# A non-local attention block: order of work in the first step of each image

## Chip, cores and metric

One core of a Trainium2 chip. The metric is the device time of one execution in microseconds (us), the median of several runs. The core has five engines that run their own instruction queues and meet at semaphores: TensorE (PE; its weight loads, PEld, are listed apart), VectorE (DVE), ScalarE (ACT), GpSimd (POOL) and SyncE (SP), which here only issues DMAs.

## The reference

Eight images `x` of 128 channels and 32 x 32 pixels, so N = 1024 tokens. Three 1x1 convolutions to 64 channels, attention without a scale over the tokens of one image, a 1x1 convolution back to 128 channels, batch normalisation with fixed statistics, and a residual:

```python
g     = (einsum('bchw,oc->bhwo', x, w_g) + b_g).reshape(B, N, Ci)
theta = (einsum('bchw,oc->bhwo', x, w_theta) + b_theta).reshape(B, N, Ci)
phi   = (einsum('bchw,oc->bohw', x, w_phi) + b_phi[:, None, None]).reshape(B, Ci, N)
att   = softmax(einsum('bnc,bcm->bnm', theta, phi), axis=-1)
y     = einsum('bnm,bmc->bnc', att, g).reshape(B, H, W, Ci)
out   = einsum('bhwc,oc->bohw', y, w_out) + b_out[:, None, None]
inv   = bn_gamma / sqrt(bn_var + 1e-5)
return x + out * inv[:, None, None] + (bn_beta - bn_mean * inv)[:, None, None]
```

## The kernel before

**Tiles.** The attention is worked in 64 tiles of 128 query rows, 8 per image (`MT = 8`); a half is four tiles (512 columns, one PSUM bank). A tile's row of 1024 scores is held in one of two double banks `ps_scores`. Per tile: `scores` (L727) makes it with four matmuls from parts of theta and phi that are stored as high and low (`theta_hl`, `phi_hh`, `phi_ll`); VectorE takes the negated row maximum (`row_maximum`, L591, and for three tiles of eight a small addition, L596); ScalarE takes the exponential with that bias and sums the row (L544, `probs`, a ring of four). Then the tile has to be transposed and split in a high and a low fp16 part, `pt_hi` and `pt_lo`. Tiles at places 1, 5 and 7 of an image are split by GpSimd (L422, L426) and transposed by DMA (`turn_hi`, `turn_lo`, L302 and L311). The other five are transposed by TensorE with the identity into two banks `ps_flip` (L792, eight transposes), and read from there by ScalarE, which writes the high part in two instructions (L532), and by VectorE, which writes the low part in two (L692: scaled source minus high part).

**Per half.** `sum_high` (L739, eight matmuls) and `sum_low` (L746, eight) accumulate attention times g in `ps_y`. VectorE scales the sum to `y_norm` (`scale_y`, L608), TensorE multiplies it by the output weights (`convolve`, L753, into `ps_misc`), VectorE adds the residual (`add_residual`, L601), and SP stores.

**Per image, for the next image.** theta and phi are projected in two halves into the same bank `ps_misc` (L826, three matmuls each, at j = 0 and 1). ScalarE takes each out to `qk` (L518, at j = 1 and 2, semaphore `proj_out`); the second projection waits for the first evacuation. GpSimd splits `qk` (L402, L407) and SP restacks the parts with six DMAs (L292). g is projected at j = 4 (L711); its largest value is spread over the partitions by a transpose (L733, at j = 7) and read by VectorE at j = 0 (L585), and small operations make scales of it (L664 to L670). At j = 0 VectorE also inverts the row sums of a half (L635) and scales two of them (L639).

**Order.** Every compute engine has a function `step(it, k)`, called for k = 0, 1, ... up to the last tile and a few steps on, with `j = k % 8`; in step k TensorE makes scores of tile k + 1 and transposes tile k - 2, ScalarE takes the exponential of tile k and the high parts of tile k - 2, and VectorE the maximum of tile k + 1 and the low parts of tile k - 2. The queues are in order, and the order inside a step is the order in which `step` lists the work. Steps 8 to 55 are a loop of three turns of 16 steps, which so begin at images 1, 3 and 5. GpSimd has its own function of the same kind. SP issues by a list written out per image (`image`).

**In the first step of an image (j = 0)**, tile k is tile 0 of the new image and tile k - 2 is tile 6 of the one before. ScalarE: high parts of tile 6 once TensorE has transposed it, then the exponential of tile 0. VectorE: the peak, the sums, the scales, the low parts of tile 6, the maximum of tile 1. TensorE: transposes of tile 6, scores of tile 1, first projection. At j = 1: scores of tile 2 (they wait for exponential 0, as the two are in the same banks: `wait(pe, probs_ready, t - 1)`), second projection, `sum_low` of the last image's first half. At j = 2: transposes of tile 0 (they wait for the low parts of tile 6: `wait(pe, pt_lo_ready, 2 * f + c - 1)`), scores of tile 3, `convolve`.

Of the kernel before, what the change touches and what calls it, by code (L numbers as in the profile page):

```python
# [23 lines left out]
def build_nonlocal_attention(nc, x, w_tp_t, w_g_t, w_out_t, channel_vectors, out):  # L24
# [9 lines left out]
    ALU = mybir.AluOpType  # L34
    ACT = mybir.ActivationFunctionType
# [5 lines left out]
    P = 128  # L41
    BANK = 512
    EPS = 1e-5
    PROB_SCALE = 2.0 ** 15
# [27 lines left out]
    with ExitStack() as ctx:  # L72
# [152 lines left out]
        def by_dma(it, k):  # L225
            return k % MT in BY_DMA and not in_last_half(tile_at(it, k))
# [257 lines left out]
        @block.scalar  # L484
        def _(act):
            def evacuate_g(b, source, target):
                wait(act, g_split, b - 1)
                nc.scalar.activation(target, source, ACT.Copy).then_inc(g_out, 1)

            def scale_y(h, r, source, cols):  # L490
                act.wait_ge(y_ready, h + 1)
                nc.scalar.activation(y_norm[:, cols], source, ACT.Copy,
                                     scale=y_unit[:, r:r + 1]).then_inc(y_scaled, 1)

            act.dma_start(w_tp[:, :], w_tp_t).then_inc(w_tp_in, 16)
# [12 lines left out]
            act.wait_ge(g_ready, 1)  # L508
            evacuate_g(0, ps_flip[0][:, :], g_raw[0][:, :, :].rearrange("p t c -> p (t c)"))

            def step(it, k):
                image, j = image_at(it, k), k % MT

                if j in (1, 2) and exists(image + 1, B):
                    c = j - 1
                    act.wait_ge(proj_ready, 2 * image + c + 1)
                    wait(act, lo_ready, 2 * image)
                    nc.scalar.activation(qk[:, c * BANK:(c + 1) * BANK], ps_misc[:, :], ACT.Identity,  # L518
                                         bias=BIAS_TP).then_inc(proj_out, 1)

                if j == 5 and exists(image + 1, B):
                    act.wait_ge(g_ready, image + 2)
                    evacuate_g(image + 1, ps_misc[:, :], g_raw[(k // MT + 1) % 2][:, :, :].rearrange("p t c -> p (t c)"))

                t = tile_at(it, k - 2)
                if exists(t, TILES) and not by_dma(it, k - 2):
                    slot, ring = (k - 2) % HALF_TILES, (k - 2) // HALF_TILES % 2
                    if slot == 0:
                        wait(act, y_ready, half_at(it, k - 2) - 1)
                    for c in range(2):  # L530
                        act.wait_ge(flipped, 2 * flip_at(it, k - 2) + c + 1)
                        nc.scalar.activation(  # L532
                            pt_hi[ring][:, c * HALF_TILES:(c + 1) * HALF_TILES, slot * P:(slot + 1) * P],
                            ps_flip[c][:, :].rearrange("p (a n) -> p a n", n=P),
                            ACT.Copy, scale=PROB_SCALE).then_inc(pt_hi_ready, 1)

                t = tile_at(it, k)
                if exists(t, TILES):
                    act.wait_ge(max_ready, t + 1)
                    if by_dma(it, k - PROB_RING):  # L540
                        wait(act, p_lo_ready, move_at(it, k - PROB_RING) + 1)
                    else:
                        wait(act, flipped, 2 * flip_at(it, k - PROB_RING) + 2)
                    nc.scalar.activation(probs[k % PROB_RING][:, :], ps_scores[k % 2][:, :], ACT.Exp,  # L544
                                         bias=neg_max[:, k % STEPS:k % STEPS + 1],
                                         accum_out=row_sum[:, k % STEPS:k % STEPS + 1]).then_inc(probs_ready, 1)

            run_steps(act, step)
            act.wait_ge(conv_ready, HALVES - 1)
            scale_y(HALVES - 1, 1, ps_y[:, LAST_PIECES[0]], LAST_PIECES[0])  # L550
            scale_y(HALVES, 1, ps_scores[0][:, 0:P], LAST_PIECES[1])

        @block.vector
        def _(dve):
# [49 lines left out]
            def scale_y(h, half, r, image, spread):  # L604
# [13 lines left out]
            nc.vector.scalar_tensor_tensor(out=SHIFT, in0=BIAS_SUM, scalar=INV, in1=BETA_SHIFT,  # L618
                                           op0=ALU.mult, op1=ALU.add).then_inc(shift_ready, 1)

            def step(it, k):
                image, j = image_at(it, k), k % MT

# [58 lines left out]
                                                   scalar=g_factor[:, 0:1], in1=g_parts[0][:, :, 0:CI],  # L682
                                                   op0=ALU.mult, op1=ALU.subtract).then_inc(g_split, 1)

                t = tile_at(it, k - 2)
                if exists(t, TILES) and not by_dma(it, k - 2):
                    slot, ring = (k - 2) % HALF_TILES, (k - 2) // HALF_TILES % 2
                    for c in range(2):
                        where = (slice(None), slice(c * HALF_TILES, (c + 1) * HALF_TILES),
                                 slice(slot * P, (slot + 1) * P))  # L690
                        dve.wait_ge(pt_hi_ready, 2 * flip_at(it, k - 2) + c + 1)
                        nc.vector.scalar_tensor_tensor(  # L692
                            out=pt_lo[ring][where], in0=ps_flip[c][:, :].rearrange("p (a n) -> p a n", n=P),
                            scalar=PROB_SCALE, in1=pt_hi[ring][where],
                            op0=ALU.mult, op1=ALU.subtract).then_inc(pt_lo_ready, 1)
                t = tile_at(it, k + 1)
                if exists(t, TILES):
                    row_maximum(it, k + 1)

            run_steps(dve, step)  # L700
            dve.wait_ge(resid_ready, B)
# [5 lines left out]
        def _(pe):  # L707
# [68 lines left out]
            def step(it, k):  # L776
# [18 lines left out]
                        last.then_inc(flipped, 1)  # L795

                h, quarter = half_at(it, k - 6), (k - 6) % HALF_TILES
                if quarter == 1 and exists(h, HALVES - 2):
                    ring, r = ring_of(k - 6), (k - 6) // MT % 2
                    pe.wait_ge(pt_lo_ready, 2 * flip_at(it, k - 7 + HALF_TILES))  # L800
                    pe.wait_ge(hi_moved[ring], moved_by(it, k - 6))
                    pe.wait_ge(g_split, image_at(it, k - 6) + 1)
                    wait(pe, y_scaled, h)
                    sum_high(ring, r, ps_y, slice(0, BANK), slice(0, BANK))

                t = tile_at(it, k + 1)
                if exists(t, TILES):
                    scores(t, it, k + 1)


                image, j = image_at(it, k), k % MT
                more = exists(image + 1, B)
                if j in (0, 1) and more:
                    if j == 0:
# [24 lines left out]
                    wait(pe, result_ready, 2 * image - 1)  # L839
                    project_g(ps_misc, (k // MT + 1) % 2, range(MT)).then_inc(g_ready, 1)  # L840


                h, quarter = half_at(it, k - 6), (k - 6) % HALF_TILES
                if exists(h, HALVES - 2):
                    ring, r = ring_of(k - 6), (k - 6) // MT % 2
                    if quarter == 3:
                        pe.wait_ge(lo_moved[ring], moved_by(it, k - 6))
                        sum_low(ring, r, ps_y, slice(0, BANK), slice(0, BANK))

                if tile_is(it, k, 1):  # L850
                    spread_peak(0, 0, ps_y[:, 0:P])
# [58 lines left out]
```

## Time and profile before

| | us |
|---|---|
| median of 3 runs | 208.63 (208.4 to 208.84) |
| the profiled execution | 210.12 |
| its span | 208.2 |
| PE busy | 196.0 (94%) |
| DVE busy | 178.3 (86%) |
| ACT busy | 136.3 (65%) |
| POOL busy | 152.5 (73%) |
| DMA, mean | 169 GB/s |

The span is the part of the profiled execution from its first to its last instruction; all rows below are times within it. The granted TensorE clock is full throughout (0.997 in the mean).

How to read it: a busy share is a mean over stages, and TensorE's ends are modelled. A row of the timeline has its start, its duration (of all instructions merged in it), engine, line, operation, output and inputs, shapes, count, and in brackets the idle time of that engine ahead of it with what ended the idle time. The chain is the work that ended last, followed back from the last instruction.

### The profile page before, as it was taken

How to read it: one execution, taken by the hardware profiler on the slowest of the kernel's cores; microseconds unless marked ns; L12 is line 12 of the kernel's file. 1: busy time of each engine (PE TensorE's matmuls, PEld its weight loads, DVE VectorE, ACT ScalarE, POOL GpSimd, SP SyncE). 2: the span in 40 equal slices, each digit the busy share in tenths (PEclk: the TensorE clock that was granted, in tenths of full speed). 3: DMA queues.
4: the chain of work that ended last, by engine and by line, in shares of the span. 5: the costliest groups of instructions: out<-in, count | busy, mean ns of one | idle time of the engine just before them, and what ended most of it. 6: DMA issues, size and time to landing. Idle time of an engine off the chain costs nothing.

```text
span 208.2 us, 3966 instructions
## 1 busy us (share of the span) xinstructions
PE 196.0 (94%) x1100; PEld 133.4 (64%) x1100; DVE 178.3 (86%) x291; ACT 136.3 (65%) x245; POOL 152.5 (73%) x127
## 2 busy tenths in 40 slices
PE   7997999999999989899999999999999998999993
PEld 6575765695666746477566856677566955566542
DVE  0689899979997898988997899878998899989861
ACT  2766867867676655676577766766577666667721
POOL 2538898699779996499987999699888965864400
PEclk9999999999999999999999999999999999999998
DMA  5215978999999999899979987899988997839211
GB/s 162 85 51 161 215 149 128 250 223 179 217 113 248 210 141 200 97 279 207 223 171 261 229 196 161 189 233 211 159 191 180 219 169 159 150 55 135 70 41 63
DMA packets 59500, 35.28 MB, mean 169 GB/s; under 512 B 50400, under 2 KB 50912, under 8 KB 59488
## 3 DMA queue, kind: packets, MB, share of 16 engines
q1 hardware_dynamic: 59200, 35.01, 81.9%
q10 hardware_dynamic: 288, 0.14, 0.2%
q14 instruction: 7, 0.06, 0.2%
q8 instruction: 5, 0.08, 0.2%
HBM read 8.36 MB, written 4.23 MB: 60 GB/s over the span
## 4 chain that ended last, share of the span: by engine, by line
PE 60%; DVE 17%; issue 7%; ACT 6%; DMA 5%; SPq 1%; POOL 1%; ACTq 0%; DVEq 0%; POOLq 0%
PE ps_scores L727 18%; PE ps_y L739 11%; PE ps_flip L792 10%; DVE neg_max L591 6%; PE ps_misc L753 6%; PE ps_misc L711 5%; DVE pt_lo L692 5%; PE ps_y L746 5%; DMA pt_hi<-p_hi 4%; ACT probs L544 4%; PE ps_scores L765 2%; DMA w_tp<-w_tp_t_dram 2%; ACT pt_hi L532 2%; PE ps_misc L826 1%; DVE y_norm L608 1%
## 5 line engine op out<-in xcount | busy, mean ns | idle before, releaser
L544 ACT ACTIVATE probs<-ps_scores,neg_max 128x1024 f32<-128x1024 f32 x64 | 71.7, 1120 | 34.3 <-DVE neg_max L596 25.5
L591 DVE TENSOR_REDUCE neg_max<-ps_scores 128x1 f32<-128x1024 f32 x64 | 78.0, 1218 | 8.9 <-PE ps_scores L727 8.4
L692 DVE SCALAR_TENSOR_TENSOR pt_lo<-ps_flip,pt_hi 128x512 f16<-128x512 f32 x84 | 53.9, 684 | 5.6 <-ACT pt_hi L532 5.4
L532 ACT ACTIVATE pt_hi<-ps_flip 128x512 f16<-128x512 f32 x84 | 45.7, 596 | 17.2 <-PE ps_flip L792 17.1
L727 PE MATMUL ps_scores<-phi_hh,theta_hl 128*128 128x512 f32 x128 | 47.1, 449 | 5.1 <-ACT probs L544 5.1
L426 POOL TENSOR_TENSOR p_lo<-probs,p_hi 128x1024 f16<-128x1024 f32 x22 | 47.0, 2138 | 4.3 <-POOL p_hi L422 3.4
L792 PE MATMUL ps_flip<-ident,probs 128*128 128x128 f32 x336 | 45.0, 276 | 0.9 <-DVE pt_lo L692 0.7
L792 PEld LDWEIGHTS ps_flip<-ident,probs 128*128 128x128 f32 x336 | 37.2, 142 | 11.2 <-issue 5.7
L727 PE MATMUL ps_scores<-phi_ll,theta_hl 128*128 128x512 f32 x128 | 40.0, 394 | 0.0
L739 PE MATMUL ps_y<-pt_hi,g_parts 128*128 128x512 f16 (+1 forms) x128 | 29.8, 376 | 0.6 <-DMA pt_hi<-p_hi 0.6
L422 POOL TENSOR_SCALAR p_hi<-probs 128x1024 f16<-128x1024 f32 x22 | 23.5, 1070 | 8.3 <-ACT probs L544 8.3
L727 PEld LDWEIGHTS ps_scores<-phi_hh,theta_hl 128*128 128x128 f32 x128 | 20.4, 190 | 11.5 <-ACT probs L544 9.3
L727 PEld LDWEIGHTS ps_scores<-phi_ll,theta_hl 128*128 128x128 f32 x128 | 24.0, 188 | 5.6
L739 PEld LDWEIGHTS ps_y<-pt_hi,g_parts 128*128 128x128 f16 x128 | 12.4, 98 | 20.1 <-issue 6.7
L469 POOL TENSOR_TENSOR x_lo<-x_in,x_hi 128x512 fp32r<-128x512 f32 x14 | 17.9, 1285 | 0.8
L407 POOL TENSOR_TENSOR lo<-qk,hi 128x512 fp32r<-128x512 f32 x14 | 17.6, 1278 | 0.8
L608 DVE SCALAR_TENSOR_TENSOR y_norm<-ps_y,y_unit,inv_all 128x512 f32<-128x512 f32 x15 | 17.1, 1142 | 1.2 <-PE ps_y L746 0.8
L402 POOL TENSOR_SCALAR hi<-qk 128x1024 fp32r<-128x1024 f32 x7 | 7.4, 1051 | 13.2 <-ACT qk L518 13.2
L753 PE MATMUL ps_misc<-y_norm,wout 128*128 128x512 f32 x30 | 16.2, 620 | 0.7 <-DVE y_norm L608 0.7
L746 PE MATMUL ps_y<-pt_lo,g_parts 128*64 128x512 f16 (+1 forms) x128 | 16.7, 382 | 0.0
L711 PEld LDWEIGHTS ps_misc<-wg,x_in 128*128 128x128 f32 x112 | 13.6, 191 | 0.6
L711 PE MATMUL ps_misc<-wg,x_in 128*128 128x64 f32 x112 | 13.2, 271 | 0.0
(80 smaller groups left out, 175.5 us busy)
## 6 DMA issues: line engine op xcount, KB each, us to landing
x_in<-x_in_dram SPq DMA_DIRECT2D x16, 256.0 KB, 3.3
inv_all<-inv_row SPq DMA_DIRECT2D x15, 256.0 KB, 4.0
out_dram<-resid SPq DMA_DIRECT2D x15, 256.0 KB, 3.0
phi_hh<-hi SPq DMA_DIRECT2D x14, 256.0 KB, 5.3
phi_ll<-lo SPq DMA_DIRECT2D x14, 256.0 KB, 5.7
theta_hl<-hi SPq DMA_DIRECT2D x7, 256.0 KB, 4.5
theta_hl<-lo SPq DMA_DIRECT2D x7, 256.0 KB, 5.5
pt_hi<-p_hi SPq DMA_TRANSPOSE x22, 4.5
```

The lines of the kernel that those rows point to most:

```text
L422: nc.gpsimd.tensor_scalar(out=high[:, :], in0=p[:, :], scalar1=1.0, scalar2=0.0, op0=ALU.mult, op1=ALU.add).then_inc(p_hi_ready, 1)
L426: nc.gpsimd.tensor_tensor(low[:, :], p[:, :], high[:, :], ALU.subtract).then_inc(p_lo_ready, 1)
L532: nc.scalar.activation(pt_hi[ring][:, c * HALF_TILES:(c + 1) * HALF_TILES, slot * P:(slot + 1) * P], ps_flip[c][:, :].rearrange("p (a n) - ...
L544: nc.scalar.activation(probs[k % PROB_RING][:, :], ps_scores[k % 2][:, :], ACT.Exp, bias=neg_max[:, k % STEPS:k % STEPS + 1], accum_out=ro ...
L591: nc.vector.tensor_reduce(out=top, in_=ps_scores[k % 2][:, :], op=ALU.max, axis=AX.X, negate=True).then_inc(row_max_ready if by_dma(it, k) ...
L692: nc.vector.scalar_tensor_tensor(out=pt_lo[ring][where], in0=ps_flip[c][:, :].rearrange("p (a n) -> p a n", n=P), scalar=PROB_SCALE, in1=p ...
L711: last = nc.tensor.matmul(target[:, m * CI:(m + 1) * CI], x_in[r][:, m * P:(m + 1) * P], wg[:, :], start=True, stop=True)
L727: last = nc.tensor.matmul(ps_scores[k % 2][:, cc], theta_hl[r][:, cols], phi[:, cc], start=(n == 0), stop=(n == 1))
L739: nc.tensor.matmul(target[:, to], g_parts[r][:, m, :], pt_hi[ring][:, m, cols], start=(m == 0), stop=False, skip_group_check=True)
L746: last = nc.tensor.matmul(target[side * CI:(side + 1) * CI, to], g_parts[r][:, m, 0:CI], pt_lo[ring][:, m, cols], start=False, stop=(m >= ...
L753: nc.tensor.matmul(target, wout[:, 0:C], y_norm[:, cols], start=True, stop=True).then_inc(conv_ready, 1)
L792: last = nc.tensor.transpose(ps_flip[c][:, a * P:(a + 1) * P], probs[(k - 2) % PROB_RING][:, m * P:(m + 1) * P], ident[:, :])
```

## The change

Three engines are reordered; no instruction is added, taken out or resized.

- ScalarE: at j = 0 the exponential of tile k goes ahead of the high parts of tile k - 2. At other j the order stays.
- VectorE: at j = 0 the maximum of tile k + 1 goes ahead of the low parts of tile k - 2. At other j the order stays.
- TensorE: `sum_low` moves from behind the projections, `convolve` and `project_g` of its step to directly behind `scores`. It falls on j = 1 and j = 5; at j = 5 nothing stood between, so only j = 1 changes, where it now stands ahead of the second projection.

```diff
 # ScalarE
+            def high_parts(it, k):
...
+            def exponential(it, k):
...
+                if j == 0:
+                    exponential(it, k)
+                high_parts(it, k)
+                if j != 0:
+                    exponential(it, k)
 # VectorE
+            def low_parts(it, k):
...
+            def next_maximum(it, k):
+                if exists(tile_at(it, k + 1), TILES):
+                    row_maximum(it, k + 1)
...
+                if j == 0:
+                    next_maximum(it, k)
+                low_parts(it, k)
+                if j != 0:
+                    next_maximum(it, k)
 # TensorE
                 if exists(t, TILES):
                     scores(t, it, k + 1)
 
+                if quarter == 3 and exists(h, HALVES - 2):
+                    pe.wait_ge(lo_moved[ring], moved_by(it, k - 6))
+                    sum_low(ring, r, ps_y, slice(0, BANK), slice(0, BANK))
+
                 more = exists(image + 1, B)
                 if j in (0, 1) and more:
...
-                h, quarter = half_at(it, k - 6), (k - 6) % HALF_TILES
-                if exists(h, HALVES - 2):
-                    ring, r = ring_of(k - 6), (k - 6) // MT % 2
-                    if quarter == 3:
-                        pe.wait_ge(lo_moved[ring], moved_by(it, k - 6))
-                        sum_low(ring, r, ps_y, slice(0, BANK), slice(0, BANK))
```

The bodies of `high_parts`, `exponential` and `low_parts` are the code that stood in `step` before.

## Rows read from the trace of the kernel before

**Rows 1.** Windows by image: span, then each engine's busy us, clock, DMA share.

```profile
78.60:103.10 24.50, 23.30 (x132) 15.72 (x130) 22.79 (x34) 15.55 (x28) 19.15 (x16) 1.00 0.97 200
...
126.46:150.31 23.85, 23.36 (x131) 15.87 (x131) 21.29 (x34) 16.17 (x30) 20.97 (x17) 1.00 0.93 190
150.31:173.67 23.36, 23.12 (x131) 15.83 (x131) 21.03 (x34) 16.17 (x30) 16.74 (x14) 1.00 0.97 193
```

**Rows 2.** Chain that ended last, at the seam b6: start, us, what.

```profile
149.38 0.93 PE ps_scores L727 x4
...
152.10 1.22 ACT probs L544 x2
153.36 1.19 PE ps_scores L727 x4
154.55 0.70 PE ps_misc L826 x3
155.25 0.98 PE ps_y L746 x8
...
158.18 0.86 PE ps_misc L753 x2
```

**Rows 3.** Timeline of the same seam, b6.

```profile
150.35 1.23 DVE L591 TENSOR_REDUCE neg_max<-ps_scores 128x1 f32<-128x1024 f32 x1
...
151.13 1.08 ACT L532 ACTIVATE pt_hi<-ps_flip 128x512 f16<-128x512 f32 x2 [0.30 <-PE ps_flip L792]
...
151.83 0.62 PE L727 MATMUL ps_scores<-phi_ll,theta_hl 128*128 128x512 f32 x2
151.89 0.17 DVE L639 TENSOR_SCALAR inv_sum<-inv_sum 128x2 f32<-128x2 f32 x1
...
152.05 2.15 POOL L426 TENSOR_TENSOR p_lo<-probs,p_hi 128x1024 f16<-128x1024 f32 x1
...
152.22 0.14 DVE L670 TENSOR_SCALAR y_unit<-g_unit 128x1 f32<-128x1 f32 x1
152.28 1.28 DVE L692 SCALAR_TENSOR_TENSOR pt_lo<-ps_flip,pt_hi 128x512 f16<-128x512 f32 x2
...
153.19 0.70 ACT L518 ACTIVATE qk<-ps_misc,vec 128x512 f32<-128x512 f32 x1
153.36 0.30 PEld L727 LDWEIGHTS ps_scores<-phi_hh,theta_hl 128*128 128x128 f32 x2 [0.65 <-ACT probs L544]
153.36 0.72 PE L727 MATMUL ps_scores<-phi_hh,theta_hl 128*128 128x512 f32 x2 [0.21 <-ACT probs L544]
...
156.36 1.16 DVE L608 SCALAR_TENSOR_TENSOR y_norm<-ps_y,y_unit,inv_all 128x512 f32<-128x512 f32 x1 [0.31 <-PE ps_y L746]
...
161.73 1.22 DVE L591 TENSOR_REDUCE neg_max<-ps_scores 128x1 f32<-128x1024 f32 x1 [1.16 <-PE ps_scores L727]
```

**Rows 4.** Timeline at the seam b3.

```profile
80.01 2.14 POOL L426 TENSOR_TENSOR p_lo<-probs,p_hi 128x1024 f16<-128x1024 f32 x1 [0.28 <-POOL p_hi L422]
80.18 1.99 DVE L639 TENSOR_SCALAR inv_sum<-inv_sum 128x2 f32<-128x2 f32 x1
...
86.10 1.12 DVE L608 SCALAR_TENSOR_TENSOR y_norm<-ps_y,y_unit,inv_all 128x512 f32<-128x512 f32 x1
```

**Rows 5.** Timeline: high sum in image 2, output product in image 3, seam b4.

```profile
75.78 1.90 PE L739 MATMUL ps_y<-pt_hi,g_parts 128*128 128x512 f16 x8 [0.57 <-DMA pt_hi<-p_hi]
...
99.32 1.12 PE L753 MATMUL ps_misc<-y_norm,wout 128*128 128x512 f32 x2
...
109.16 1.14 DVE L608 SCALAR_TENSOR_TENSOR y_norm<-ps_y,y_unit,inv_all 128x512 f32<-128x512 f32 x1
```

**Rows 6.** Chain at the seam b4: what follows the output product.

```profile
111.83 1.73 PE ps_y L739 x8
```

**Rows 7.** Timeline at the seam b7.

```profile
176.91 0.73 PE L727 MATMUL ps_scores<-phi_hh,theta_hl 128*128 128x512 f32 x2 [0.90 <-ACT probs L544]
...
179.64 1.16 DVE L608 SCALAR_TENSOR_TENSOR y_norm<-ps_y,y_unit,inv_all 128x512 f32<-128x512 f32 x1 [0.27 <-issue]
```

More of the change, by code:

```diff
@@ L509, in _ @@
             evacuate_g(0, ps_flip[0][:, :], g_raw[0][:, :, :].rearrange("p t c -> p (t c)"))
+            def high_parts(it, k):
+                t = tile_at(it, k - 2)
+                if exists(t, TILES) and not by_dma(it, k - 2):
+                    slot, ring = (k - 2) % HALF_TILES, (k - 2) // HALF_TILES % 2
+                    if slot == 0:
+                        wait(act, y_ready, half_at(it, k - 2) - 1)
+                    for c in range(2):
+                        act.wait_ge(flipped, 2 * flip_at(it, k - 2) + c + 1)
+                        nc.scalar.activation(
+                            pt_hi[ring][:, c * HALF_TILES:(c + 1) * HALF_TILES, slot * P:(slot + 1) * P],
+                            ps_flip[c][:, :].rearrange("p (a n) -> p a n", n=P),
+                            ACT.Copy, scale=PROB_SCALE).then_inc(pt_hi_ready, 1)
+            def exponential(it, k):
+                t = tile_at(it, k)
+                if exists(t, TILES):
+                    act.wait_ge(max_ready, t + 1)
+                    if by_dma(it, k - PROB_RING):
+                        wait(act, p_lo_ready, move_at(it, k - PROB_RING) + 1)
+                    else:
+                        wait(act, flipped, 2 * flip_at(it, k - PROB_RING) + 2)
+                    nc.scalar.activation(probs[k % PROB_RING][:, :], ps_scores[k % 2][:, :], ACT.Exp,
+                                         bias=neg_max[:, k % STEPS:k % STEPS + 1],
+                                         accum_out=row_sum[:, k % STEPS:k % STEPS + 1]).then_inc(probs_ready, 1)
             def step(it, k):
@@ L523, in step @@
                     evacuate_g(image + 1, ps_misc[:, :], g_raw[(k // MT + 1) % 2][:, :, :].rearrange("p t c -> p (t c)"))
[L525 to L546, printed above, removed]
+                if j == 0:
[3 more added lines that the diff above has]
+                    exponential(it, k)
             run_steps(act, step)
@@ L619, in _ @@
                                            op0=ALU.mult, op1=ALU.add).then_inc(shift_ready, 1)
+            def low_parts(it, k):
+                t = tile_at(it, k - 2)
+                if exists(t, TILES) and not by_dma(it, k - 2):
+                    slot, ring = (k - 2) % HALF_TILES, (k - 2) // HALF_TILES % 2
+                    for c in range(2):
+                        where = (slice(None), slice(c * HALF_TILES, (c + 1) * HALF_TILES),
+                                 slice(slot * P, (slot + 1) * P))
+                        dve.wait_ge(pt_hi_ready, 2 * flip_at(it, k - 2) + c + 1)
+                        nc.vector.scalar_tensor_tensor(
+                            out=pt_lo[ring][where], in0=ps_flip[c][:, :].rearrange("p (a n) -> p a n", n=P),
+                            scalar=PROB_SCALE, in1=pt_hi[ring][where],
+                            op0=ALU.mult, op1=ALU.subtract).then_inc(pt_lo_ready, 1)
+            def next_maximum(it, k):
+                if exists(tile_at(it, k + 1), TILES):
+                    row_maximum(it, k + 1)
             def step(it, k):
@@ L683, in step @@
                                                    op0=ALU.mult, op1=ALU.subtract).then_inc(g_split, 1)
[L685 to L698, printed above, removed]
+                if j == 0:
[3 more added lines that the diff above has]
+                    next_maximum(it, k)
             run_steps(dve, step)
@@ L797, in step @@
                 h, quarter = half_at(it, k - 6), (k - 6) % HALF_TILES
+                ring, r = ring_of(k - 6), (k - 6) // MT % 2
                 if quarter == 1 and exists(h, HALVES - 2):
-                    ring, r = ring_of(k - 6), (k - 6) // MT % 2
                     pe.wait_ge(pt_lo_ready, 2 * flip_at(it, k - 7 + HALF_TILES))
@@ L808, in step @@
                     scores(t, it, k + 1)
-                image, j = image_at(it, k), k % MT
+                if quarter == 3 and exists(h, HALVES - 2):
+                    pe.wait_ge(lo_moved[ring], moved_by(it, k - 6))
+                    sum_low(ring, r, ps_y, slice(0, BANK), slice(0, BANK))
                 more = exists(image + 1, B)
@@ L840, in step @@
                     project_g(ps_misc, (k // MT + 1) % 2, range(MT)).then_inc(g_ready, 1)
-                h, quarter = half_at(it, k - 6), (k - 6) % HALF_TILES
-                if exists(h, HALVES - 2):
-                    ring, r = ring_of(k - 6), (k - 6) // MT % 2
-                    if quarter == 3:
-                        pe.wait_ge(lo_moved[ring], moved_by(it, k - 6))
-                        sum_low(ring, r, ps_y, slice(0, BANK), slice(0, BANK))
                 if tile_is(it, k, 1):
```

## The prediction

> **What bounds the kernel.** I read the windows by image first, then the chain that ended last, then the timeline at the seam of two images, then the same seam elsewhere. I write b1 to b7 for the first step of images 1 to 7 (j = 0), and "tile 0, 1, 2, 6, 7" for a tile's place in its image. The windows run from the end of tile 0's scores to the same point one image later. TensorE is busy 23.12 of 23.36 us of the b6 image, VectorE 21.03 and GpSimd at most 20.97 [rows 1]. So an image is a run of TensorE work, and only what makes TensorE wait can be won. The chain shows where: in the b6 image it lies on TensorE nearly throughout, except at the seam, where it leaves for ScalarE's exponential (152.10, 1.22 us) and comes back as scores of 1.19 us, where undisturbed scores take 0.93 [rows 2]. The timeline shows that TensorE had nothing for 0.21 us before them, and its weight load for 0.65 us [rows 3]. What is won there stays won if nothing later in the image is waiting on another clock: VectorE idles 1.16 us for tile 4's scores [rows 3], so it catches up by then.
>
> **Part 1, ScalarE: the exponential of tile 0 ahead of tile 6's high parts.** Nothing is added. The maximum of tile 0 ends at 150.35 + 1.23 = 151.58; the high parts (151.13, 1.08) stand in front, so the exponential starts at 152.10 [rows 3]. After the change it starts at about 151.62 and ends 1.22 later, at 152.84, not 153.32: 0.48 earlier. The first projection's last matmul ends at 153.36 - 0.21 = 153.15 [rows 3]. The stall is therefore gone: tile 2's scores end at 153.15 + 0.93 = 154.08 instead of 153.36 + 1.19 = 154.55, which is 0.47 us earlier (0.21 idle and 0.26 of filling). The trace shows the weight load starting at 153.36, together with the stalled matmul and not ahead of it. The Trainium skill (TensorE: Matmul & The Clock Gate, Step-by-step: what each phase is for) says that weight loads are pulled ahead of matmuls in flight; by that rule the refill would cost nothing and each seam would return only the idle 0.21. The row goes against it for a load whose own inputs are already there, since the wait stands ahead of the load.
>
> **What becomes late.** The high parts now run 152.84 to 153.92, and the first evacuation of the projections (0.70, begun at 153.19 before [rows 3]) ends at about 154.6 instead of 153.89. The second projection waits for it. In the old order TensorE would be ready for that projection at 154.08 and stand for some 0.5 us, more than was won.
>
> **Part 2, TensorE: the low half ahead of the second projection.** This covers the wait: eight low matmuls take 0.98 us [rows 2], so the projection comes up at 154.08 + 0.98 = 155.06, after 154.6. No instruction is added. I cost the swap at nothing; if switching operand kinds costs more on one side, it is a tenth or two, in either direction. The projection ends at about 155.8 rather than 155.25, so the second evacuation ends near 156.6, where it used to wait for tile 1's exponential anyway; GpSimd's split and the restacking DMAs behind it on the SP queue, and the transposing DMA behind those, move by less than 0.3 us. SP's own order is untouched. Tile 0 is not transposed by DMA, so no queue sees that exponential directly.
>
> **Part 3, VectorE: the maximum of tile 1 ahead of tile 6's low parts.** With the low parts first, VectorE would wait for high parts that now come 0.8 us later. The maximum fills that gap. It needs tile 1's scores, done at 151.83 + 0.62 = 152.45, while VectorE's small operations end at 152.36 [rows 3]: some 0.1 us idle. Low parts, two maxima and the small addition took from 152.28 to 156.36 - 0.31 = 156.05 before [rows 3], 3.77 us; the same four in the new order, from 152.49, end at 156.26. The scaled sum (1.16, 156.36) so starts at about 156.2, close to where it did. This limits the gain: the output product waits for it. A product that comes up to a scaled sum just finished takes 1.12 [rows 5] from 0.06 after it. At b6 that is 156.2 + 1.16 + 0.06 + 1.12 = 158.54, against 158.18 + 0.86 = 159.04 [rows 2]: 0.50, so TensorE's 0.47 is the smaller and counts. At b4 VectorE had no idle time, the sum keeps its end at 109.16 + 1.14 = 110.30, and the product ends at 111.48 instead of 111.83 [rows 5, 6]: 0.35. The low parts end near 155.1; the transposes of tile 0, which overwrite what they read, come up at 155.8: hidden, by 0.7 us.
>
> **The two odd seams.** At b3 the scaling of the sums (128x2) took 1.99 us where its work is a fraction: it ends at 82.17, just as GpSimd's low part does (80.01 + 2.14 = 82.15). The scaled sum then ends at 86.10 + 1.12 = 87.22 [rows 4], all of it VectorE's queue, which the change does not shorten: I take 0.05 there. The Trainium skill (SBUF — State Buffer, SBUF: two separate sides) calls the port that VectorE and GpSimd share an exclusive lock held for a whole instruction; the row agrees, and the rule is what the rival on the slow side rests on. At b7 there is no projection, and TensorE stood 0.90 us, from 176.01 to 176.91 [rows 7]. That stall goes, but tile 1's maximum can only begin at 176.05, so the four operations end at 179.82 and the scaled sum starts at about 179.8 instead of 179.64 [rows 7]. The whole gain is handed back to the output product, with 0.1 us on top. Image 0 has no tile 6 before it and no low half, and the steps behind the last tile have no exponential: no change there.
>
> **Sum.** Five usual seams (b1, b2, b4, b5, b6) at the mean of 0.35 and 0.47, about 0.4 each, 2.0; b3 0.05; b7 -0.1: about 1.95 of the profiled execution's 210.12 us (span 208.2), so 208.2. That execution is 1.49 above the median of 208.63. Its b3 image took 24.50 against 23.85 for the b5 image, which begins a loop turn as well [rows 1]; before it a matmul waited 0.57 for a transposing DMA [rows 5]. That is 1.22 of the 1.49, so I take it that the usual run has neither, and b3 is a usual seam. Then six times 0.4 less 0.1 is 2.3: 208.63 - 2.3 = **206.3 us**. 0.2% (0.4 us) is about what a measurement of this kernel can tell from none.
>
> **Rivals.**
> *Half of it.* Either the refill was hidden anyway, so a seam returns 0.21 (six times, less 0.1: 1.2, giving 207.4), or VectorE's queue ends later than I lay it out and the product swallows all but 0.1 to 0.2 a seam, giving 207.9. For it: b7, where that happens in full. Against it: the margins at b5 and b6. Chance 0.17.
> *No difference.* TensorE's stall reappears as a wait for y_norm at each seam, or the transposing DMA for the high sum, already late once [rows 5], takes up the lead: 208.2 to 209.0. Chance 0.10.
> *More.* The scaled sum never binds and b7 keeps its 0.9: six times 0.47 and 0.9, 3.7, giving 204.9. Against it: the arithmetic of b7. Chance 0.05.
> *Slower: the collision of b3 spreads.* The scaling of the sums is issued 0.16 us before GpSimd's 2.15 us low part of tile 7 begins (151.89, 152.05 [rows 3]). If TensorE's spread of the peak, and with it VectorE's small operations, comes over 0.16 us later against GpSimd than now, VectorE stands 2 us at the head of the step, with tile 1's maximum behind it. That image costs 0.65 [rows 1] and loses its 0.4. It decides from three seams on: 2.3 - 3 x 1.05 = -0.85, giving 209.5. For it: a margin of 0.16. Against it: nothing in step 7, where both begin, is moved, and GpSimd rather gets later against TensorE, away from it. Chance 0.10.
> *My forecast* has 0.58, with a range of its own of 205.6 to 207.1.
>
> **Numbers.** Faster by over 0.2%: 0.58 + 0.05 + 0.13 of the half case, 0.76. Within 0.2%: 0.09 + 0.04, 0.13. Slower: 0.10 + 0.01, 0.11. The range 205.2 to 208.3 holds the forecast, the half case and part of the even one; the slow rival, the rest of the even one and most of the high gain are left out, some 2 in 10.
>
> **What would show it.** Right: at b1 to b6 tile 2's scores take 0.93 with no idle time ahead, exponential 0 starts within 0.1 us of its maximum's end, the second projection follows the low half at once, and the output product now waits for y_norm for 0.2 us or less; at b7 it waits 0.5 or more; the b6 image is near 23.0 and ScalarE's share of the chain at the seams is gone. Wrong: idle time ahead of the second projection or of tile 0's transposes (part 2 too short), a scaling of 2 us at several seams, or images still at 23.36.

## The result and the profile after

The changed kernel takes 207.06 us in the median of 22 runs (205.9 to 209.12), the kernel before 208.61 in 22 runs beside them (208.4 to 210.35). The medians are 1.55 us (0.7%) apart; 2.3 had been forecast (206.3, within 205.2 to 208.3). The ratio of the means is 0.9932, 95% interval 0.9911 to 0.9954, or 1.4 us; it leaves out the two slowest runs of the changed kernel, which count as slow ones. The runs of the changed kernel lie in two groups with nothing between them: twelve from 205.9 to 207.13 (median 206.5) and ten from 208.41 to 209.12 (median 208.7). The profiled execution, at 208.85 with a span of 207.0, is of the upper group. So two things are to be explained: what the reordering is worth in an image, and what the upper group is.

Line numbers after the change: scores L743, transposes L808, projections L844, low sum L762, output product L769, spread of the peak L749, exponential L532, high parts L519, evacuation L543, maximum L599, low parts L637, scaled sum L616, scaling of the sums L664.

Windows by image of the kernel after, from the spread of the peak (which follows tile 0's scores at once) to the next one; columns as in [rows 1]. The images are b6, b5, b1 and b4:

```profile
149.53:172.49 22.96, 22.94 (x131) 15.87 (x131) 21.00 (x34) 16.06 (x30) 17.36 (x14) 1.00 0.95 185
126.11:149.53 23.42, 23.15 (x131) 15.94 (x131) 21.15 (x34) 16.16 (x30) 20.21 (x17) 1.00 0.92 200
32.57:56.76 24.19, 23.54 (x132) 15.67 (x130) 22.28 (x34) 15.56 (x28) 20.16 (x16) 1.00 0.98 191
103.17:126.11 22.94, 22.91 (x132) 15.83 (x132) 21.14 (x34) 16.07 (x30) 20.22 (x17) 1.00 0.91 205
```

b6 went from 23.36 to 22.96 and b5 from 23.85 to 23.42 [rows 1]; b4, which took 23.36 before as well, to 22.94. TensorE is now busy for 22.94 of 22.96. The chain of the kernel after at the seam b6, start, us, what:

```profile
149.86 0.87 PE ps_flip L808 x8
150.73 0.93 PE ps_scores L743 x4
151.66 0.71 PE ps_misc L844 x3
152.37 0.93 PE ps_scores L743 x4
153.30 0.98 PE ps_y L762 x8
154.28 0.89 PE ps_misc L844 x3
155.16 0.87 PE ps_flip L808 x8
156.04 0.93 PE ps_scores L743 x4
156.97 0.86 PE ps_misc L769 x2
```

ScalarE's 1.22 us are gone from it [rows 2]. Tile 2's scores take 0.93 and follow the first projection at once. The second projection now takes 0.89 and the transposes 0.87 where they took 0.70 and 1.02: what follows the low sum is the longer one by 0.15 to 0.19, in either order. The timeline of the same seam:

```profile
149.55 1.23 DVE L599 TENSOR_REDUCE neg_max<-ps_scores 128x1 f32<-128x1024 f32 x1
...
150.81 1.11 ACT L532 ACTIVATE probs<-ps_scores,neg_max 128x1024 f32<-128x1024 f32 x1 [0.78 <-DVE neg_max L599]
...
151.70 1.22 DVE L599 TENSOR_REDUCE neg_max<-ps_scores 128x1 f32<-128x1024 f32 x1
...
152.87 0.70 ACT L543 ACTIVATE qk<-ps_misc,vec 128x512 f32<-128x512 f32 x1
...
153.07 1.29 DVE L637 SCALAR_TENSOR_TENSOR pt_lo<-ps_flip,pt_hi 128x512 f16<-128x512 f32 x2
...
155.41 1.16 DVE L616 SCALAR_TENSOR_TENSOR y_norm<-ps_y,y_unit,inv_all 128x512 f32<-128x512 f32 x1
```

Exponential 0 starts 0.03 us after its maximum's end (149.55 + 1.23 = 150.78). The scaled sum ends at 156.57, before TensorE comes up to the product at 156.97 by the chain (156.81 in its timeline).

At b7 nothing is won. Timeline of the kernel after:

```profile
172.49 0.32 PE L749 MATMUL ps_misc<-ident,g_peak 128*128 128x128 f32 x1
...
174.84 1.22 DVE L599 TENSOR_REDUCE neg_max<-ps_scores 128x1 f32<-128x1024 f32 x1 [0.32 <-PE ps_scores L743]
...
175.03 0.74 PE L743 MATMUL ps_scores<-phi_hh,theta_hl 128*128 128x512 f32 x2 [0.23 <-ACT probs L532]
...
179.77 1.10 PE L769 MATMUL ps_misc<-y_norm,wout 128*128 128x512 f32 x2 [0.60 <-DVE y_norm L616]
```

TensorE's wait for the exponential fell from 0.90 [rows 7] to 0.23, but the product now waits 0.60 for the scaled sum. From the spread to the end of the product are 8.38 us (172.49 to 179.77 + 1.10), as before (173.69 to 182.05, 8.36).

**Where the rest went.** Against the trace of before, with the spread of the peak as mark, image b1 took 24.19 for 23.82, b2 23.11 for 23.91, b3 23.30 for 24.68, b4 to b6 0.42, 0.43 and 0.40 less, and b7 with the tail 34.5 in both: together 3.06 us less. But b1 began at 32.57 instead of 30.71, 1.86 later, after a start and an image 0 in which the change alters nothing: image 0's own spread came at 15.63 instead of 15.23, and from there image 0 took 16.94 instead of 15.48. The difference, 1.2, is that of the spans. Image 0 and the next seam in the kernel after:

```profile
29.91 1.89 PE L755 MATMUL ps_y<-pt_hi,g_parts 128*128 128x512 f16 x8 [1.31 <-DVE pt_lo L637]
...
32.57 0.27 PE L749 MATMUL ps_misc<-ident,g_peak 128*128 128x128 f32 x1
...
33.65 2.15 POOL L426 TENSOR_TENSOR p_lo<-probs,p_hi 128x1024 f16<-128x1024 f32 x1
...
34.30 1.52 DVE L664 TENSOR_SCALAR inv_sum<-inv_sum 128x2 f32<-128x2 f32 x1
...
40.97 1.12 PE L769 MATMUL ps_misc<-y_norm,wout 128*128 128x512 f32 x2 [0.60 <-DVE y_norm L616]
```

The high sum waited 1.31 us. The row names VectorE's low part, but the last one that this sum needs (tile 3's) was written at 26.96, and in the trace of before the same sum began ahead of tile 4's. So it was the other wait ahead of it, the transposing DMA of tile 1: issued at 22.42, it landed 7.4 us later, at 29.8. TensorE came 1.3 us late to the seam against GpSimd, and VectorE's scaling met GpSimd's low part and ended with it (35.82 and 35.80). These are the late DMA of image 2 and the stretch at b3 in the trace of before [rows 4, 5], two images earlier.

### The profile page after: what moved, and what is told of

It is laid out like the page before. It is cut to its first block, busy times and chain, and to the rows that moved or that the text cites. A ratio compares the mean times of both kernels' runs of the same rounds, so it can differ in the third digit from the quotient of the medians.

```text
span 207.0 us, 3966 instructions
## 1 busy us (share of the span) xinstructions
PE 195.8 (95%) x1100; PEld 133.6 (65%) x1100; DVE 176.9 (85%) x291; ACT 136.5 (66%) x245; POOL 152.4 (74%) x127
## 3 DMA queue, kind: packets, MB, share of 16 engines
HBM read 8.36 MB, written 4.23 MB: 61 GB/s over the span
## 4 chain that ended last, share of the span: by engine, by line
PE 69%; DVE 19%; issue 5%; ACT 2%; DMA 2%; DVEq 0%; ACTq 0%
PE ps_scores L743 20%; PE ps_flip L808 12%; PE ps_y L755 12%; DVE neg_max L599 7%; PE ps_misc L769 6%; DVE pt_lo L637 6%; PE ps_misc L727 6%; PE ps_y L762 5%; PE ps_misc L844 4%; DVE y_norm L616 3%; PE ps_scores L781 2%; DMA w_tp<-w_tp_t_dram 2%; ACT pt_hi L519 1%; PE ps_flip L727 1%; DVE inv_sum L664 1%
## 5 line engine op out<-in xcount | busy, mean ns | idle before, releaser
L532 ACT ACTIVATE probs<-ps_scores,neg_max 128x1024 f32<-128x1024 f32 x64 | 71.7, 1121 | 33.7 <-DVE neg_max L599 16.5
L599 DVE TENSOR_REDUCE neg_max<-ps_scores 128x1 f32<-128x1024 f32 x64 | 78.0, 1219 | 11.1 <-PE ps_scores L743 10.6
L637 DVE SCALAR_TENSOR_TENSOR pt_lo<-ps_flip,pt_hi 128x512 f16<-128x512 f32 x84 | 54.0, 685 | 5.0 <-ACT pt_hi L519 5.0
L519 ACT ACTIVATE pt_hi<-ps_flip 128x512 f16<-128x512 f32 x84 | 45.6, 595 | 13.4 <-PE ps_flip L808 13.4
L743 PE MATMUL ps_scores<-phi_hh,theta_hl 128*128 128x512 f32 x128 | 46.5, 444 | 2.1 <-ACT probs L532 2.0
L808 PE MATMUL ps_flip<-ident,probs 128*128 128x128 f32 x336 | 44.8, 276 | 1.1 <-DVE pt_lo L637 0.7
L808 PEld LDWEIGHTS ps_flip<-ident,probs 128*128 128x128 f32 x336 | 37.6, 142 | 9.9 <-issue 3.5
L743 PE MATMUL ps_scores<-phi_ll,theta_hl 128*128 128x512 f32 x128 | 40.1, 394 | 0.0
L755 PE MATMUL ps_y<-pt_hi,g_parts 128*128 128x512 f16 (+1 forms) x128 | 29.8, 376 | 1.5 <-DVE pt_lo L637 1.3
L743 PEld LDWEIGHTS ps_scores<-phi_ll,theta_hl 128*128 128x128 f32 x128 | 24.0, 188 | 5.6
L743 PEld LDWEIGHTS ps_scores<-phi_hh,theta_hl 128*128 128x128 f32 x128 | 20.7, 190 | 6.3 <-ACT probs L532 3.8
L769 PE MATMUL ps_misc<-y_norm,wout 128*128 128x512 f32 x30 | 16.3, 624 | 1.9 <-DVE y_norm L616 1.9
L616 DVE SCALAR_TENSOR_TENSOR y_norm<-ps_y,y_unit,inv_all 128x512 f32<-128x512 f32 x15 | 17.1, 1141 | 0.0
L762 PE MATMUL ps_y<-pt_lo,g_parts 128*64 128x512 f16 (+1 forms) x128 | 16.7, 382 | 0.0
```

Source lines behind the costliest of these rows:

```text
L519: nc.scalar.activation(pt_hi[ring][:, c * HALF_TILES:(c + 1) * HALF_TILES, slot * P:(slot + 1) * P], ps_flip[c][:, :].rearrange("p (a n) - ...
L599: nc.vector.tensor_reduce(out=top, in_=ps_scores[k % 2][:, :], op=ALU.max, axis=AX.X, negate=True).then_inc(row_max_ready if by_dma(it, k) ...
L637: nc.vector.scalar_tensor_tensor(out=pt_lo[ring][where], in0=ps_flip[c][:, :].rearrange("p (a n) -> p a n", n=P), scalar=PROB_SCALE, in1=p ...
L743: last = nc.tensor.matmul(ps_scores[k % 2][:, cc], theta_hl[r][:, cols], phi[:, cc], start=(n == 0), stop=(n == 1))
L755: nc.tensor.matmul(target[:, to], g_parts[r][:, m, :], pt_hi[ring][:, m, cols], start=(m == 0), stop=False, skip_group_check=True)
L762: last = nc.tensor.matmul(target[side * CI:(side + 1) * CI, to], g_parts[r][:, m, 0:CI], pt_lo[ring][:, m, cols], start=False, stop=(m >= ...
```

## Experiments

Each kernel is the changed one with the edit shown, unless it says otherwise; medians are of its timed runs beside runs of the kernel before on the same chip.

**The changed kernel again**, twice (no edit).

> The changed kernel once more, unaltered. Its timed runs lie in two groups, 205.9 to 207.1 and 208.4 to 209.1 us. Theory (a transposing DMA that lands late in an image, after which the scaling of two sums meets GpSimd's low part of tile 7 and stands for 1.5 to 2 us): both groups again, 2.0 to 2.4 apart, and in this profile the step j = 7 of each image either has a high sum that waits for a DMA and then a long scaling (span about 207), or has neither (span about 204.5). Rival (the two groups come from something spread over all images): the images from b4 to b7 take other times than 22.96 and 23.4 us.

207.59 us (12 runs: six from 206.13 to 206.8, six from 208.39 to 209.08) against 208.91, ratio 0.992 (0.988 to 0.996). The profile (209.08) is of the upper group: the high sum of image 0 waited 1.72 us, the next scaling took 1.12, and b1 began at 33.24. b4 to b7 are as in the first trace.

> The changed kernel a third time, beside the three below on one chip. Theory: two groups again, near 206.3 and 208.5, with the high group in a quarter to a half of the runs; where the profile is of the high group, one image has a late transposing DMA and, in the next, a stretched scaling. Rival (the high group is of one chip or one program load): runs of one group alone.

206.7 us (six runs from 205.99 to 206.78, one at 208.53) against 208.61, ratio 0.9885 (0.9854 to 0.9916). This profile (208.53) departs from the theory: image 0 waited 0.43, image 1 0.24 for a transposing DMA, and no scaling met a low part (the longest took 0.36). It was late before that: its scores just ahead of g's projection began at 22.73, where they began at 21.19 in the trace of before. The delay arose in TensorE's first eight projection matmuls, here the row of before and then that of this run:

```profile
4.89 3.77 PE L765 MATMUL ps_scores<-x_in,w_tp 128*128 128x512 f32 x8
```

```profile
5.07 5.27 PE L781 MATMUL ps_scores<-x_in,w_tp 128*128 128x512 f32 x8
```

TensorE has no idle time inside either row. The median of their weight loads is 0.34 us in this run and 0.19 in the trace of before; the granted clock reads 1.00 in both. It was not a wait for the image: GpSimd, which needs all of it, had begun at 7.99. The same matmuls took 4.53 and 4.49 us in the first two profiles of the changed kernel. So the upper group has no single cause. Against the trace of early_turn (below), which nothing disturbed, the three profiles are late by 0.45, 0.71 and 1.58 at the first spread, by 1.48, 1.89 and 0.60 more in image 0, and by 0.77, 0.37 and 0.06 more in image 1.

Over the three sets 17 of 41 runs are in the upper group; of the kernel before, 13 of 80 are at 209.8 or above.

**No swap on TensorE.**

```diff
-                if quarter == 3 and exists(h, HALVES - 2):
-                    pe.wait_ge(lo_moved[ring], moved_by(it, k - 6))
-                    sum_low(ring, r, ps_y, slice(0, BANK), slice(0, BANK))
                 more = exists(image + 1, B)
...
+                if quarter == 3 and exists(h, HALVES - 2):
+                    pe.wait_ge(lo_moved[ring], moved_by(it, k - 6))
+                    sum_low(ring, r, ps_y, slice(0, BANK), slice(0, BANK))
```

> The changed kernel with TensorE's order as before: the low sum stays behind the second projection. ScalarE and VectorE keep the new order. Theory: the second projection comes up before the first evacuation has ended and TensorE stands 0.4 to 0.6 us ahead of it at each of six seams; the b6 image takes 23.4 to 23.5 us instead of 22.96, and the kernel 208.5 to 209.5 in its usual runs. Rival (the swap on TensorE is not needed): no wait ahead of the second projection, the image stays at 22.96, the kernel at 206.5.

209.51 us, ratio 1.0036 (1.0003 to 1.0068): the gain is gone. Timeline at b6, and its window:

```profile
153.41 0.47 PE L840 MATMUL ps_misc<-x_hi,w_tp_hi 128*128 128x512 f32 x1 [0.43 <-ACT qk L543]
```

```profile
149.25:172.81 23.56, 23.11 (x131) 15.80 (x131) 21.16 (x34) 16.14 (x30) 16.71 (x13) 1.00 1.02 202
```

TensorE stands 0.43 for the first evacuation; the image takes 23.56. Without TensorE's swap the gain is not there.

**No swap on VectorE.**

```diff
-                if j == 0:
-                    next_maximum(it, k)
                 low_parts(it, k)
-                if j != 0:
-                    next_maximum(it, k)
+                next_maximum(it, k)
```

> The changed kernel with VectorE's order as before: low parts of tile 6 ahead of the maximum of tile 1. ScalarE and TensorE keep the new order. Theory: VectorE waits 0.6 to 0.8 us for the high parts, which now come after the exponential, the scaled sum ends that much later, and the output product at j = 2 waits for it 0.5 to 0.8 us longer than in the changed kernel; the b6 image takes 23.4 to 23.7, the kernel 208.5 to 210. Rival (the maximum's place does not matter): the image stays at 22.96.

210.47 us, ratio 1.0093 (1.0042 to 1.0144), b6 23.69. VectorE waits for the high parts as expected, but the place where TensorE pays is another one:

```profile
152.73 1.29 DVE L637 SCALAR_TENSOR_TENSOR pt_lo<-ps_flip,pt_hi 128x512 f16<-128x512 f32 x2 [0.61 <-ACT pt_hi L519]
```

```profile
156.71 0.73 PE L740 MATMUL ps_scores<-phi_hh,theta_hl 128*128 128x512 f32 x2 [0.48 <-ACT probs L532]
```

The late maximum of tile 1 makes exponential 1 late, and tile 3's scores wait 0.48 for that; the product at 157.75 then does not wait.

**TensorE's swap alone** (ScalarE and VectorE as before).

> The kernel before with TensorE's swap alone (the low sum ahead of the second projection; ScalarE and VectorE as before). Theory: nothing on TensorE waits for what is moved earlier, so the b6 image stays at 23.36 within 0.1 and the kernel within 0.4 us of 208.6. Rival (the earlier low sum itself brings the gain): 23.0 per image and about 206.5.

209.12 us, ratio 1.0013 (0.9985 to 1.004), and at b6:

```profile
149.54:172.96 23.42, 23.20 (x131) 15.84 (x132) 21.01 (x34) 16.17 (x30) 17.33 (x14) 1.00 0.91 184
```

Nothing, as expected. So TensorE's swap alone gives nothing, and with either cover taken away the kernel is no faster than before. ScalarE's swap and VectorE's were not run alone.

**Scaling split.** Where the scaling has two sums (128x2), two instructions on one each; where it has one, nothing changes.

```diff
-                        moved = inv_sum[:, cols.start + slots[0]:cols.start + slots[-1] + 1:2]
-                        nc.vector.tensor_scalar(out=moved, in0=moved, scalar1=PROB_SCALE, scalar2=None,
-                                                op0=ALU.mult).then_inc(inv_sum_ready, 1)
+                        for slot in slots:
+                            moved = inv_sum[:, cols.start + slot:cols.start + slot + 1]
+                            last = nc.vector.tensor_scalar(out=moved, in0=moved, scalar1=PROB_SCALE,
+                                                           scalar2=None, op0=ALU.mult)
+                        last.then_inc(inv_sum_ready, 1)
```

> The changed kernel; the scaling of two sums at j = 0 (128x2, every second element) is two instructions on one element each. Theory (a lock between VectorE and GpSimd that this form alone asks for; the 128x1 forms in the trace never stretch): both instructions take about 0.15 us in every image, also where GpSimd is at work on the same memory, so that an image 0 with a late transposing DMA costs its own wait alone (1.3 to 1.7) and not 0.6 to 0.9 on top. Two groups of runs again, 1.3 to 1.7 apart instead of 2.2; the lower near 206.2. Rival (the stretch comes from the data or from any instruction there): one of the two takes 0.3 to 2 us where the one did.

206.03 us (205.94 to 207.23, 6 runs) against 208.7, ratio 0.9864 (0.9823 to 0.9905). The pair takes 0.21 or 0.22 us at each of the seven seams, where the one instruction took 0.74 at b1 and 0.30 to 0.37 at b2 to b5 even in the undisturbed trace of early_turn. Such short stretches cost nothing that can be seen: b1 took 23.42 us there and 23.39 here. No run of the upper group fell here; six runs are few for that. This trace, undisturbed, has b1 beginning at 30.51 and b6 at 22.93.

> The kernel before with the split scaling alone. Theory: in its usual runs the stretch (0.3 to 0.7 us) is hidden behind TensorE's own stall for ScalarE, so they stay at 208.3 to 208.7; the rare runs at 210 and above come down by some 0.7. Rival (the scaling alone brings what the changed kernel with it had won over the changed kernel): usual runs at 208.0 or less.

208.76 us (208.29 to 209.41, 12 runs) against 208.61, ratio 0.9997 (0.9979 to 1.0016): the split alone is worth nothing in usual runs. None of the 12 is above 209.8. Its profile has a late DMA in image 2, 0.76 us, and no stretch after it:

```profile
75.93 1.90 PE L741 MATMUL ps_y<-pt_hi,g_parts 128*128 128x512 f16 x8 [0.76 <-DMA pt_hi<-p_hi]
...
80.34 0.21 DVE L640 TENSOR_SCALAR inv_sum<-inv_sum 128x1 f32<-128x1 f32 x2
```

The next image took 23.34 us there (78.60 to 101.94), against 24.68 in the trace of before, where the stretch followed.

**Transposing DMA first.**

```diff
                     restack(phi_hh[1 - r], CI, hi, CI, 1 - r)
+                    turn_hi(MT * b + 1)
                     sp.wait_ge(lo_ready, 2 * b + 2)
...
-                turn_hi(MT * b + 1)
+                else:
+                    turn_hi(MT * b + 1)
```

> The changed kernel; on SP the transposing DMA of tile 1's high part goes ahead of the three restacking DMAs of the low parts. Theory (the high group of runs is that DMA landing late in image 0, behind 768 KB of restacking): it is issued up to 1 us earlier and lands 2 us or more earlier, no high sum waits for it, and the group at 208.4 to 209.1 is gone; what may come instead is a wait for the restacked parts ahead of tile 0's scores, in image 0 above all, as they land 3 to 4 us later and had 1 to 3 us to spare. Net 205.9 to 208.5. Rival (the two groups do not hang on this DMA): both groups stay, 2 us apart.

206.3 us (205.93 to 206.47, and one run at 207.75) against 208.7, ratio 0.9871 (0.9828 to 0.9915). In image 0 the DMA lands in 3.7 us, against 7.4, 7.8 and 6.5 in the three traces of the changed kernel, and no scores wait for restacked parts. No run at 208.4, but again six runs, and one near 207.8.

**Scaled sum early in the last image.**

```diff
+                if j == 1 and exists(image, B) and not exists(image + 1, B):
+                    scale_y(half_at(it, k - 9), 0, (k - 9) // MT % 2, image_at(it, k - 9),
+                            it * (8 * STEPS // HALF_TILES) + 16 * ((k - 9) // MT + 1))
                 if j != 0:
                     next_maximum(it, k)
```

(and at j = 2 it is left out for that image)

> The changed kernel; in the last image alone VectorE makes the scaled sum at the end of j = 1, ahead of the maximum of tile 2, instead of at j = 2 behind it. Theory (in the last image the whole gain at the seam is given back to the output product, which stands 0.60 us for the scaled sum): that wait goes, the product ends 0.7 to 0.9 earlier, and the kernel gains 0.6 to 0.9 in either group of runs, 205.5 in the lower. Rival (what is won there is lost at the next exponential, which now comes 1.1 later): no gain, and a wait of scores for an exponential at tile 4 or 5 of the last image.

206.79 us, three runs from 205.48 to 206.17 and three from 207.4 to 207.91. The medians of the two groups, 205.9 and 207.5, are 0.6 and 1.2 below those of the changed kernel, from three runs each. The product's wait at b7 is gone. Its profile is of the upper group, with the late DMA in image 1; the whole mechanism in rows:

```profile
52.61 1.90 PE L758 MATMUL ps_y<-pt_hi,g_parts 128*128 128x512 f16 x8 [0.90 <-DMA pt_hi<-p_hi]
...
56.57 2.15 POOL L426 TENSOR_TENSOR p_lo<-probs,p_hi 128x1024 f16<-128x1024 f32 x1 [0.29 <-POOL p_hi L422]
...
57.02 1.73 DVE L664 TENSOR_SCALAR inv_sum<-inv_sum 128x2 f32<-128x2 f32 x1
58.97 1.22 DVE L599 TENSOR_REDUCE neg_max<-ps_scores 128x1 f32<-128x1024 f32 x1
...
62.67 1.15 DVE L616 SCALAR_TENSOR_TENSOR y_norm<-ps_y,y_unit,inv_all 128x512 f32<-128x512 f32 x1
63.87 1.13 PE L772 MATMUL ps_misc<-y_norm,wout 128*128 128x512 f32 x2 [0.61 <-DVE y_norm L616]
```

Windows of that image, b2, and of b4 in the same trace:

```profile
55.28:79.67 24.39, 23.78 (x133) 15.52 (x131) 22.48 (x34) 15.57 (x28) 20.18 (x16) 1.00 0.97 191
103.13:126.09 22.96, 22.95 (x132) 15.86 (x132) 21.15 (x34) 16.07 (x30) 20.21 (x17) 1.00 0.94 200
```

The scaling ends with GpSimd's instruction (58.75 and 58.72), and everything behind it on VectorE is 1.4 to 1.5 us late; the image takes 24.39, 1.43 more than an undisturbed one of its kind.

**The versions that beat both kernels.** Early scaled sum and split scaling together, twice:

> The changed kernel with both the early scaled sum in the last image and the split scaling of the sums. Theory: the two gains add, 0.6 to 0.9 in every run and another 0.6 to 0.9 in the runs of the high group: groups at about 205.5 and 207. Rival: as the changed kernel, 206.3 and 208.5.

205.28 us (204.98 to 205.67, 6 runs) against 208.7, ratio 0.9811 (0.9773 to 0.9849).

> The fastest kernel of this study again: the changed kernel with the early scaled sum in the last image and the split scaling. Theory: 205.0 to 205.8 in most runs, and no run above 207.5, since a late transposing DMA now costs 1 to 1.7 us alone; 1.5% under the kernel before. Rival (its six runs happened to miss the high group): a third of the runs at 207.5 and more.

205.74 us (205.38 to 206.03, and one at 207.2) against 208.61, ratio 0.9857 (0.982 to 0.9894). With the transposing DMA first as well:

> The same with the transposing DMA of tile 1 ahead of the restacking of the low parts. Theory: the late DMA no longer costs anything, so the runs draw together at 205.0 to 205.8. Rival (the restacked low parts now land late now and then, ahead of tile 0's scores): the spread stays or grows, and the profile shows a wait for a restacking DMA.

205.25 us (204.97 to 205.57) against 208.61, ratio 0.9827 (0.9797 to 0.9856), with no wait for a restacking DMA: the narrowest spread of all, though the intervals of the three overlap.

## Why the prediction was right, and by how much it was off

**Parts 1 to 3 held.** The exponential starts 0.03 us after its maximum; tile 2's scores take 0.93 with no idle time; the second projection comes up after the evacuation (153.57); an image gains 0.40 to 0.43 where "about 0.4" had been taken. The refill of 0.26 came back with the idle 0.21: an image gains more than 0.21 alone can give. That is as the row said; by what the prediction took from the Trainium skill (TensorE: Matmul & The Clock Gate, Step-by-step: what each phase is for), that weight loads are pulled ahead, only the 0.21 would have come. Taking each cover away brought the waits: 0.43 for part 2 (forecast 0.5), and 0.61 on VectorE for part 3. There the prediction let the high parts come 0.8 us later; by its own rows it is 1.7 (151.13 and 152.84), and nothing in the sum hung on it. ScalarE's swap was neither run alone nor taken out alone; what it does is read from the traces.

**The cap by the scaled sum was set slightly too low.** At b4 it was to limit the gain to 0.35; there the gain is 0.42, and the product does not wait at b2 to b6. The prediction let the scaled sum at b4 keep its end; it started 0.16 earlier after the spread, since the scaling of the sums took 0.37 where it had 0.58 in the trace of before. At b7 it takes the whole gain, as forecast (8.38 against 8.36; 0.1 worse was forecast), and moving the scaled sum showed that the cap is the cause: 0.75 us between the medians of split_scale and early_sum_split.

**The sum held for the undisturbed run and failed for the median.** The lower group's median, 206.5, is 2.1 below 208.6, where 2.3 was forecast. The step that failed is "I take it that the usual run has neither" the late DMA nor the stretch. In the kernel before, 67 of 80 runs are below 209.8. In the changed kernel the upper group holds 10 of the 22 timed runs, and that alone moves the median from 206.5 to 207.06, which is nearer to the 207.4 of the rival "half of it" than to the forecast. The traces exclude that rival's two mechanisms: the refill came back, and the product does not wait at b2 to b6. That the median fell inside the range was in part luck: with two more of the 22 runs in the upper group it would have been above 208.3.

**The price of a stretch was set too low, as the slow rival had it.** It was given 0.65 of its own, from 24.50 for the b3 image of before against 23.85 for b5, both of which begin a loop turn. But b5 has a stall that b3 has not. At b5 TensorE waits for ScalarE soon after the turn, and the image takes some 0.5 longer than b6. In the trace of before:

```profile
127.06 1.09 PE L792 MATMUL ps_flip<-ident,probs 128*128 128x128 f32 x8 [0.26 <-ACT probs L544]
```

In an image that begins late this is absent. The b3 image of before_split_scale took 23.34, and its b5 23.86. The b1 image of pe_swap_only, after a high sum that waited 0.59, took 23.37, and its b5 23.90. The high sum and the window of that b1:

```profile
28.84 1.89 PE L749 MATMUL ps_y<-pt_hi,g_parts 128*128 128x512 f16 x8 [0.59 <-issue]
```

```profile
31.50:54.87 23.37, 23.13 (x132) 15.78 (x131) 21.04 (x34) 16.27 (x30) 20.20 (x16) 1.00 1.08 200
```

So the stretch at b3 of before cost 24.68 - 23.34 = 1.34, not 0.65. In the changed kernel b2 of early_sum lost 1.43 by a scaling of 1.73. For b1 of its first two profiles no undisturbed image that began late is on record; measured against the 22.95 of an image without the turn's stall, an estimate from these rows, scalings of 1.52 and 1.12 cost 1.2 and 0.8. In the new order all but some 0.1 of what a scaling took over 0.17 came through, in the old order all but 0.5 (1.34 of 1.82). The old order had a wait for ScalarE that could hide some of it. That the new order is the more sensitive one is thus likely, but it rests on one stretched image of the old order and on that estimate. The rival itself, several seams in every run, did not occur.

In the traces a stretched scaling ends 0.01 to 0.03 us after a GpSimd instruction that was running when it began, the high part of tile 7 for those up to 0.75 us and the low part for the longer ones. The rule on the shared port (the Trainium skill, SBUF — State Buffer, SBUF: two separate sides) agrees with that. Only the 128x2 scaling was stretched; the 128x1 instructions never were, in the same place beside the same GpSimd work.

**Open.** Why the start-up and the transfers are late in some runs and not in others. The transposing DMA of image 0 landed after 5.5 to 5.8 us in the eight profiles whose image 0 was not held up and that issue it in the same place, and after 6.5 to 7.8 in four: the three of the changed kernel, and pe_swap_only, where ScalarE and VectorE keep the old order. Both profiles of the old order on all engines have one late in image 2, and one of them, before_split_scale, was a usual run at 208.82. So late DMAs are not particular to the new order, and the groups of times do not count them: one that no long stretch follows costs little (image 0 and b1 of pe_swap_only took 39.59 together, 39.30 in the trace of before). Whether they are more frequent in the changed kernel is not shown; no run here changed only the placement of the program. With the split scaling or the transposing DMA first, none of 30 runs was at 208 or above; how much of that is the edit's, these runs do not say.

## What to carry to other kernels

Moving work earlier on one engine pays only if what it overtakes is covered elsewhere: here one swap on ScalarE needed one on VectorE and one on TensorE, and without either of them the kernel was as slow as before or slower. Ask of an instruction that may stretch under contention what stands directly behind it: here 1.4 of 1.6 us came through to the end of the image. Where runs fall in groups, look at which group the profile is of before a term is blamed, and take the undisturbed image to compare with from the same situation: a stall that one image has and the other has not hid half of a price here. A two-element instruction that contended for a port was written here as two single-element ones; the pair was never stretched.

## What was not expected of the hardware

Two 128x1 scalings take 0.22 us together beside a running GpSimd instruction, where one 128x2 took 0.17 when alone and up to 1.99 when not. The transposing DMA of tile 1 in image 0, behind the same six restacking DMAs, took from 5.5 to 7.8 us to land, and 3.7 when it was issued ahead of three of them. In the first trace of the kernel after, the transfer engines moved nothing from 28.5 to 29.0 us and 6 GB/s in the half microsecond behind it, while that DMA had not landed. TensorE's first eight projection matmuls took from 3.38 to 5.27 us in the profiles, at a granted clock that reads 1.00. A TensorE group behind a semaphore wait takes 0.26 longer than one that flows (1.19 against 0.93), even after an idle time of 0.65 us on the weight load.
